# Cross-attention and feed-forward block on one core: K's low part as two 64-row matmuls in the four-batch M tiles, with the PSUM banks that this takes

## The reference, cut to what matters

```python
x = x + xattn(ctx, layernorm(x), ...)        # x (16, 1024, 512), ctx (16, 64, 512)
x = x + tanh(((layernorm(x) @ W) @ A1) @ A2 + bias)

def xattn(ctx, latents, shift, scale, ...):  # 16 heads of 64, all in float32
    kv = layernorm(ctx) @ Wkv                # k, v: 64 keys per batch
    q = (layernorm(latents) @ Wq) * (1 + scale) + shift
    attn = softmax(q @ k.T / 8)
    return (attn @ v) @ Wout
```

## Time and profile before

| | |
|---|---|
| three timed runs | 2052.75, 2054.31, 2054.54 us; median 2054.31 us |
| span of the profiled execution, first to last instruction | 2049.4 us |
| its own time | not given apart; the median of the runs is 4.9 us above the span |
| busy share of the span | PE 99%, PEld 82%, DVE 74%, ACT 64%, POOL 65% |
| granted TensorE clock, mean over the span | 0.999 |
| pieces of four batches | 96, the last one at 1474 us |

### The profile page before, as it was taken

One profiled execution on the slowest core, in us unless ns is written; L12 is line 12 of the kernel. 1 busy time (PEld: TensorE's weight loads), 2 busy tenths in 40 slices (PEclk: granted clock), 3 DMA queues, 4 the chain that ended last, 5 costly groups with the idle time before them and its releaser, 6 DMA issues.

```text
span 2049.4 us, 31334 instructions
## 1 busy us (share of the span) xinstructions
PE 2024.3 (99%) x9168; PEld 1679.8 (82%) x9168; DVE 1523.8 (74%) x2416; ACT 1320.3 (64%) x3005; POOL 1342.0 (65%) x1463
## 2 busy tenths in 40 slices
PE   8998999999999999999999999999999999999998
PEld 6887878888888888888888888888888888888887
DVE  7567777776777777677777777777777777777776
ACT  4465667666766667666666667666666666666654
POOL 2136767767676776767676776767577676767564
PEclk9999999999999999999999999999999999999999
DMA  7657978889787887878788787878767576666653
GB/s 256 196 184 219 269 226 245 247 231 253 215 229 206 222 222 209 225 202 233 195 229 223 206 224 205 229 201 216 209 186 210 175 206 181 201 184 191 178 169 118
DMA packets 502489, 431.53 MB, mean 211 GB/s; under 512 B 54832, under 2 KB 408240, under 8 KB 502320
## 3 DMA queue, kind: packets, MB, share of 16 engines
q1 hardware_dynamic: 502320, 429.54, 74.3%
HBM read 251.33 MB, written 178.06 MB: 210 GB/s over the span
## 4 chain that ended last, share of the span: by engine, by line
PE 94%; DVE 1%; DMA 1%; ACT 1%; SPq 1%; issue 1%; POOL 0%; DVEq 0%; ACTq 0%
PE bank L161 38%; PE bank L1126 23%; PE bank L166 19%; PE bank L1129 11%; PE bank L830 1%; PE bank L829 1%; DMA stage_more<-ffn_wT_dram 0%; PE bank L827 0%; SPq L306 0%; DMA kv_scratch<-area 0%; ACT bank L388 0%; DMA p_moved<-p_scratch 0%; ACT M_hi L392 0%; PE bank L511 0%; DMA p_scratch<-area 0%
## 5 line engine op out<-in xcount | busy, mean ns | idle before, releaser
L1403 POOL TENSOR_TENSOR area<-area,row_max 128x256 f32<-128x256 f32 x512 | 353.7, 711 | 147.8 <-DVE row_max L1269 147.8
L1126 PE MATMUL bank<-N_hi,pT_hi 128*128 128x512 f32 x1024 | 398.8, 389 | 3.0 <-ACT pT_hi L1172 1.7
L161 PE MATMUL bank<-M_lo,xT_hi 128*128 128x512 f32 x1024 | 398.7, 389 | 0.0
L161 PE MATMUL bank<-M_hi,xT_hi 128*128 128x512 f32 x1024 | 398.6, 389 | 0.0
L1126 PE MATMUL bank<-N_lo,pT_hi 128*128 128x512 f32 x1024 | 398.5, 389 | 0.0
L1172 ACT CAST pT_hi<-turned 128x512 fp32r<-128x512 f32 x256 | 159.1, 621 | 330.4 <-DVE turned L1286 330.4
L1410 POOL TENSOR_TENSOR area<-area,row_inv 128x512 f32<-128x512 f32 x256 | 269.0, 1051 | 114.3 <-DVE row_inv L1278 114.0
L1427 POOL TENSOR_TENSOR area<-area 128x512 f32<-128x512 f32 x127 | 166.0, 1307 | 240.6 <-ACT area L1211 240.5
L1275 DVE TENSOR_REDUCE row_sum<-area 128x8 f32<-128x512 f32 x256 | 174.4, 681 | 167.7 <-ACT area L1167 166.7
L1295 DVE TENSOR_TENSOR pT_lo<-turned,pT_hi 128x512 fp32r<-128x512 f32 x256 | 196.5, 768 | 118.0 <-ACT pT_hi L1172 117.9
L166 PE MATMUL bank<-M_hi,xT_lo 128*128 128x512 f32 x1024 | 273.8, 389 | 0.1
(11 more groups left out here) (178 smaller groups left out, 3916.8 us busy)
## 6 DMA issues: line engine op xcount, KB each, us to landing
p_scratch<-area SPq DMA_DIRECT2D x256, 256.0 KB, 2.6
p_moved<-p_scratch SPq DMA_DIRECT2D x512, 128.0 KB, 4.2
area<-x_dram SPq DMA_DIRECT2D x128, 256.0 KB, 4.5
area<-x_turned_dram SPq DMA_DIRECT2D x128, 256.0 KB, 4.0
x_scratch<-area SPq DMA_DIRECT2D x127, 256.0 KB, 3.0
x_moved<-x_scratch SPq DMA_DIRECT2D x508, 64.0 KB, 3.4
y_dram<-area SPq DMA_DIRECT2D x127, 256.0 KB, 3.4
land<-m_scratch SPq DMA_DIRECT2D x120, 256.0 KB, 2.7
```

Of the source, the lines that this page charges most:

```text
L161: mm = eng.matmul(ps, sh, mv, start=(n == 0), stop=False)
L1126: pe.matmul(O_ps[:], st(pT_hi, k), n_cols(mv, k), start=(k == 0 and mv is N_hi), stop=False)
L1403: last = pool.tensor_tensor(s, s, row.to_broadcast([P, 2, 4, J2]), ALU.subtract)
```

## The change

1. The 96 pieces of four batches take two adjoining banks, 3 and 4, one for each head. The two `k_hi` matmuls stay as they were, 128 rows by 256 columns. The two `k_lo` matmuls become 64-row matmuls: head 0 takes the partitions 0 to 63 of its stationary and moving operand, head 1 the partitions 64 to 127. For that, `wst_scratch` holds head 1's high part in the partitions 64 to 127 and its low part in 0 to 63. The product of the two low parts is dropped. The order is hi of head 0, hi of head 1, lo of head 0, lo of head 1. The pieces of two batches keep bank 4 and their two matmuls.
2. ACT's copy of such a piece reads 256 columns of each of the two banks where it read 512 of one.
3. In the 14 later folds pair 7 takes O's bank (6), not bank 3, and waits until DVE has read O of this slot (`s_x2`), not for pair 3. Pair 3 waits for the copy of the piece at place C, where there is one. Place D of the slots 17 and 25 waits for DVE's read of pair 3. O's first half in slot m = 2 waits for all eight pairs.

```diff
-        banks = [ctx.enter_context(nc.psum_tensor(f"bank{i}", [P, BANK], F32)) for i in range(8)]
+        def bank(i, n=1):
+            return ctx.enter_context(nc.psum_tensor(f"bank{i}", [P, n * BANK], F32))
+
+        low = [bank(i) for i in range(3)]
+        tile_pair = bank(3, 2)
+        banks = low + [tile_pair[:, h * BANK:(h + 1) * BANK] for h in range(2)] + [bank(i) for i in range(5, 8)]
...
-        first_fold_ps, fold_ps = [banks[i] for i in (2, 3, 7)], banks[0:4]
+        first_fold_ps, fold_ps = [banks[i] for i in (2, 3, 7)], banks[0:4] + banks[0:3] + [banks[6]]
...
-                            sp.dma_start(wst_scratch[8 * i:8 * i + 8, part * DH:(part + 1) * DH, h, :].rearrange("n e d -> e n d"),
+                            row = (part + h) % 2 * DH
+                            sp.dma_start(wst_scratch[8 * i:8 * i + 8, row:row + DH, h, :].rearrange("n e d -> e n d"),
...
                 else:
-                    pe.matmul(ps[:, own], st, k_hi[:, own], start=True, stop=False)
-                    mm = pe.matmul(ps[:, own], st, k_lo[:, own], start=False, stop=True)
+                    pe.matmul(pair_of_tile(h, nb), st, k_hi[:, own], start=True, stop=False)
+            if nb > 2:
+                for h in range(2):
+                    rows, own = slice(h * DH, (h + 1) * DH), slice(h * nb * CTX, (h + 1) * nb * CTX)
+                    mm = pe.matmul(pair_of_tile(h, nb), wst_bufs[i][rows, h * P:(h + 1) * P], k_lo[rows, own], start=False, stop=True)
             mm.then_inc(s_mt, 1)
+
+        def pair_of_tile(h, nb):
+            return tile_pair[:, h * BANK:h * BANK + nb * CTX]
...
-                     part_of_tile(1) if nb == 2 else ps.rearrange("p (h b j) -> p h b j", h=2, b=nb)).then_inc(s_tev, 1)
+                     part_of_tile(1) if nb == 2 else tile_pair[:, :].rearrange(
+                         "p (h x b j) -> p h x b j", h=2, x=2, j=CTX)[:, :, 0]).then_inc(s_tev, 1)
...
-                if p < len(use):
+                if b8:
+                    free(p)
+                    if 4 <= p < 7:
+                        pe.wait_ge(s_nl, b8 + p - 3)
+                elif p < len(use):
                     free(p)
...
-                        pe.wait_ge(s_nl, u + 4 + 4 * q)
+                        pe.wait_ge(s_nl, u + 8 if u else 4 + 4 * q)
...
-                fold_n_pe(pe, t - 1, range(8), lambda p: pe.wait_ge(s_sb[p], t + 1) if p < 2 else None)
+                def free(p):
+                    if p < 2:
+                        pe.wait_ge(s_sb[p], t + 1)
+                    if p == 3 and tile_at.get((t, "C"), 0) >= 32:
+                        pe.wait_ge(s_tev, tile_at[t, "C"] + 1)
+                    if p == 7:
+                        pe.wait_ge(s_x2, t - 1)
+                fold_n_pe(pe, t - 1, range(8), free)
+                if tile_at.get((t, "D"), 0) >= 32:
+                    pe.wait_ge(s_nl, t + 3)
```

## The result

The changed kernel takes 2081.6 us (median; 2080.6 to 2082.9) against 2054.4 us before, measured side by side: ratio 1.0132, interval 1.0120 to 1.0144. It is 27.2 us slower. The forecast was 2045.7 us, 8.6 us faster. The 27.2 us are 0.283 us for each of the 96 pieces of four batches.

What follows compares the result with a forecast made beforehand. PE was taken to bound the kernel: 2054.3 us less 8.6 (96 pieces at 0.09 us, pair overlapped, changes cheap), with copy, stores and fold at 0, gave 2045.7 us; 8-in-10 range 2042.5 to 2075.

Steps and rivals of the forecast that it cites:

- What bounds the kernel: Main loop: PE never waits for another engine, so PE time saved or added in 96 pieces counts one for one.
- Cost of a matmul: PE in a piece: 117.5 ns per 256-column matmul, with the next weight load going ahead during the matmul before.
- best bound: Pair in each piece: both matmuls run at once and row changes cost nothing, three steps not four, -11.3 us.
- second rival: Pieces on PE: loads go one after the other, or changes cost about the pair's saving; 2050.5 to 2058, chance 0.23.
- about 14 ns lost at each of the two changes: Into and out of the 64-row pair: small loss per change, leaving 90 ns saved a piece, 8.6 us.
- upper bound: Each row-mode change: array empties (177 ns) and the load is in the open (80 ns), 0.26 us each time.
- break-even of 59 ns: Price of one row-mode change, two a piece, from which the piece becomes longer: 117.5 / 2 = 59 ns.
- bound of 0 to 260: Price in ns of one row-mode change around the pair: at best 0, at most 260.
- first rival: PE, ahead of the first 64-row matmul and the following 512-column one: changes cost 80 ns or more; 2058.4 upward, chance 0.36.
- full emptying without the load: Each row-mode change costs 177 ns because the array empties: +236.5 ns a piece, +22.7 us, 2077.0.
- Copy, stores, fold: ACT's two-bank copy, setup stores of the stationary operand, and the fold's 24 matmuls: each adds 0.
- covers of 1 to 5 us: New waits in the fold, place D and O's first half: slack of 1.0 to 5.2 us, so none binds.

Runs made afterwards that it cites:

- e4: Changed kernel reordered to hi, lo of head 0, then hi, lo of head 1, giving four row-count changes a piece: 2128.5 us against 2052.8 before.
- e6: Changed kernel with the 64-row pair issued four times in a row: 2113.9 us against 2053.8 before.
- e7: Changed kernel with the k_lo pair issued four times, as 128-row matmuls: 2120.1 us against 2053.8 before.
- e8: Changed kernel with the 64-row pair in every second piece only, 128-row matmuls in the others: 2067.3 us against 2053.8 before.
- e11: Changed kernel without the product of K's low part, two 128-row matmuls a piece: 2038.2 us against 2052.8 before.
- e2: Changed kernel with both 64-row k_lo matmuls on partitions 0 to 63, so no overlap: 2090.4 us against 2052.8 before.
- e10: Changed kernel with k_lo matmuls at 128 rows but only 64 columns of the stationary operand: 2053.6 us against 2052.8 before.
- e1: Changed kernel with the two k_lo matmuls back at 128 rows; banks, copy and fold stay changed: 2053.0 us against 2052.8 before.
- e3: Changed kernel with the 64-row pair ahead of the two k_hi matmuls: 2077.4 us against 2052.8 before.
- e9: Changed kernel with the 64-row pair on only the first 64 columns of each stationary operand: 2074.7 us against 2052.8 before.

## Why the prediction was wrong

- **What bounds the kernel.** Right for the change: PE alone, and time added went one for one into the run (e4, e6, e7, e8). Wrong as "PE time taken out of a piece therefore shortens the run one for one": e11 shows that it does so in the 64 slots with one piece, while the 16 with two gave 1.2 of 7.5 us. I had compared slots with one and with none, and not looked at those with two. Had the pair worked as forecast, the gain would have been between 5.8 us (64 x 0.09) and 8.6; no run shows where.
- **Cost of a matmul and the best bound.** Right: 0.1175 us a step; the overlap is worth 10.4 us (e2), and loads in the two halves run at the same time, so the part of the second rival that has the loads one after the other is out. The Trainium skill's "TensorE: Matmul & The Clock Gate", Part 3, has row tiles start about 4 ns apart with their loads overlapping. The trace agrees: 3 ns between the starts of the pair, and one merged load of 0.19 us.
- **The step that failed: "about 14 ns lost at each of the two changes".** It is 0.20 us each: 0.10 in which nothing starts, read as the array emptying, and 0.11 for a load that nothing covers, less 0.01. Both parts stood in my upper bound (as 0.177 and 0.08). I chose near the low end with the argument that nothing in the rows makes a matmul wait for the one before it to leave the array. But every row that I had was between matmuls of the same row count, so they said nothing about a change. With a break-even of 59 ns in a bound of 0 to 260, most of the bound spoke for slower. The Trainium skill's "TensorEngine Tiling (Array Packing)", section Key Properties, says that a change of tiling mode drains TensorE. The trace agrees for the rows, with 0.10 us in which nothing starts at each change; for 64 of the 128 columns (e10) it shows no such gap.
- **The first rival** was the case, with its place right: ahead of the first 64-row matmul and ahead of the first 512-column one, 0.28 us a piece between the 0.24 and 0.40 that it named. Its chance of 0.36 was too low, and the range was cut at 2075 inside this rival, just under a full emptying without the load (2077.0); the time lies between the rival's 2077.0 and 2092.9.
- **Copy, stores, fold:** right, all at 0 (e1). The covers of 1 to 5 us held: the view of waits has none of the new ones.

## What to carry to other kernels

Row tiles pay only if enough of them stand together: count the changes of row count first, price each at two costs (0.10 us in which nothing starts and one weight load in the open, together 0.2 us here), and set against it one full step saved per pair. Here, by a straight line between one pair and four, each stretch of 64-row matmuls needs more than three pairs of 256 columns. When an operation has no row in a trace, rows of its kind without the special circumstance are no bound on it, and the end of the bound that they resemble is not the likelier one. Even the middle of this bound, 130 ns a change, gives (2 x 130 - 117.5) x 96 = 13.7 us slower: the right sign, and half of the measured loss. And before counting time taken out of the busiest engine as gained, look at every kind of slot: where another loop is as long, the gain stops there (e11).

## What the runs showed of the hardware

- Between 128-row and 64-row matmuls, in either direction, no load starts until about 0.10 us after the last columns have gone in (the change, e3, e4); then load (0.11 us for 128 columns, half of that for 64 in e9) and columns follow one after the other.
- Two 64-row loads and two 64-row matmuls in different halves, with different banks, start 3 ns apart, and a pair costs 0.114 us for 256 columns (e6). Going from one half to the other costs nothing there; in the same half, a second 64-row matmul costs 0.11 us more (e2).
- Going from 128 to 64 columns of the stationary operand and back, at 128 rows, cost nothing: +0.8 us over 96 such visits, within the interval (e10).
